# A graph network on one core: the last pass in another order, and twelve tiles kept in SBUF between two passes

## What is computed

```python
h = (x @ W.T).reshape(N, 4, 64)
e = leaky_relu(a_s[src] + a_d[dst], 0.2)        # edges and a loop at each node
p = exp(e - m[dst]);  alpha = p / (segment_sum(p, dst) + 1e-16)
out = segment_sum(alpha[:, :, None] * h[src], dst).reshape(N, 256) + bias
x = layernorm(elu(out) + x + x)
```

## Time and profile before

| | |
|---|---|
| runs of the kernel before | 5779.85 us median of 3 (5770.6 to 5787.17) |
| the profiled execution | 5752.64 us, span 5750.9 us |
| busy in the span | PE 4250.1 us, DVE 3705.5, POOL 3618.8, ACT 1959.4 |
| DMA | 1129.62 MB moved, mean 196 GB/s |
| mean granted TensorE clock | 0.873 |

### The profile page before, as it was taken

How to read it: one execution, slowest core, us unless ns; L and a number is a source line. 1 busy time by engine, 2 the same in 40 slices (tenths; PEclk the granted TensorE clock), 3 DMA queues, 4 the chain that set the end, 5 groups by cost and what they waited for, 6 DMA issues and landing times. The chain is left out here.

```text
span 5750.9 us, 69994 instructions
## 1 busy us (share of the span) xinstructions
PE 4250.1 (74%) x16758; PEld 2855.9 (50%) x16758; DVE 3705.5 (64%) x10203; ACT 1959.4 (34%) x3345; POOL 3618.8 (63%) x3319
## 2 busy tenths in 40 slices
PE   2377679999999999999999777767777400026776
PEld 1255445556666666666666566656666300012222
DVE  1255456566666666666666566668888645558887
ACT  0011145532222222222222222227777300016666
POOL 7488644433556666555555566657777776668887
PEclk7688889999999999999999887778999755559888
DMA  9988799984433333333333233339999522249997
GB/s 378 283 154 153 139 303 365 363 313 148 142 121 123 123 123 123 122 121 119 118 119 111 90 124 122 123 119 317 325 325 324 197 88 81 86 137 352 350 347 286
DMA packets 497174, 1129.62 MB, mean 196 GB/s; under 512 B 164006, under 2 KB 246906, under 8 KB 497030
## 3 DMA queue, kind: packets, MB, share of 16 engines
q1 hardware_dynamic: 331530, 866.20, 43.1%
q0 software_dynamic: 113184, 174.84, 12.5%
q10 hardware_dynamic: 52316, 87.06, 4.3%
HBM read 627.40 MB, written 543.83 MB: 204 GB/s over the span
## 5 line engine op out<-in xcount | busy, mean ns | idle before, releaser
L1067 PE MATMUL psum<-W2b,arena 128*128 128x256 f32 x3136 | 725.2, 379 | 0.0
L799 DVE TENSOR_SCALAR arena<-arena 128x256 f32<-128x256 f32 x784 | 463.0, 653 | 369.4 <-POOL arena L794 364.9
L1048 PE MATMUL psum<-arena,W1b 128*128 128x512 f32 x1568 | 699.1, 599 | 0.0
L1067 PEld LDWEIGHTS psum<-W2b,arena 128*128 128x128 f32 x3136 | 573.1, 190 | 66.3 <-issue 0.5
L1761 PE MATMUL psum<-arena,ident 128*128 128x512 f32 x784 | 418.8, 685 | 194.7 <-POOL arena L1819 192.4
L959 ACT ACTIVATE arena<-psum,hbias 128x512 f32<-128x512 f32 x392 | 269.5, 687 | 809.6 <-PE psum L1048 809.6
L1192 POOL DMA_INDIRECT tab<-arena,IDX x392 | 408.9, 1043 | 190.4 <-issue 114.0
L1610 POOL DMA_INDIRECT ad_d<-arena,FE x392 | 406.9, 1038 | 156.1 <-issue 127.4
L1048 PEld LDWEIGHTS psum<-arena,W1b 128*128 128x128 f32 x1568 | 289.8, 190 | 402.4 <-issue 402.4
L790 POOL TENSOR_TENSOR arena<-arena,lneps 128x4 f32<-128x4 f32 x196 | 42.0, 215 | 668.3 <-DVE arena L786 667.5
L1251 PE MATMUL psum<-ident,arena 128*128 128x128 f32 x24 | 5.7, 424 | 590.4 <-DVE arena L1419 581.1
(11 more groups left out here) (256 smaller groups left out, 9269.0 us busy)
## 6 DMA issues: line engine op xcount, KB each, us to landing
arena<-tab SPq DMA_DIRECT2D x194, 544.0 KB
arena<-x_d SPq DMA_DIRECT2D x202, 512.0 KB
arena<-in_x SPq DMA_DIRECT2D x194, 512.0 KB
x_d<-arena SPq DMA_DIRECT2D x194, 512.0 KB
tab<-zero SPq DMA_DIRECT2D x11, 5832.0 KB
tab<-blank SPq DMA_DIRECT2D x97, 544.0 KB
h_d<-arena SPq DMA_DIRECT2D x97, 528.0 KB
arena<-h_d SPq DMA_DIRECT2D x97, 528.0 KB
```

Source lines behind the costliest of these rows:

```text
L799: v.tensor_scalar(y[:, j, :], r[:, j, :], self.mv[:, j, 0:1], self.rs[:, j:j + 1], ALU.subtract, ALU.mult).then_inc(self.s["y"], 1)
L1048: last = pe.matmul(psum[:, HB[c], :], W1b[:, f, c * P:(c + 1) * P], x1T[:, f, :], start=False, stop=(f == FH - 1))
L1067: last = pe.matmul(outB(j), hid[:, c, j * P:(j + 1) * P], W2b[:, c, :], start=(c == 0), stop=(c == KH - 1))
```

## The change

**Kept tiles.** The weights and the two constant tiles get a place at the end of one large array, and from phase four on twelve tiles of [128, 4, 256] lie where they and some unused room were. In `edge_pass(2)` SyncE loads into tile m the x2 rows of step 8m (m = 0 to 11). `node_pass` reads the rows of these steps there and doesn't load them. In steps 8m + 4 ScalarE copies `y` into tile m, and `y` isn't stored to `x3_d`; `last_pass` reads these steps' rows from tile m and doesn't load them. The loops of these two passes get bodies of eight steps in place of four where slots of eight matter.

**The last pass in another order.** TensorE does the two matmuls of `oh`, for which it waits alone, then the two of `oS`. The residual sum `rr` has four buffers and not two. `factors` and `shares` are cut into seven pieces, `heads`, `slopes`, `maxima`, `below`, `sums`, `totals`, `shares`, which VectorE does at different places of its body. The negated mean of step k (`negated`) moves behind the elu of step k + 1.

The diff, cut to its core:

```diff
+        NKEEP, TILE = 12, J * D
+        KEEP0 = ARENA - 5 * TILE
+        arena = sb("arena", [P, KEEP0 + NKEEP * TILE + J * TW - TILE])
+        kept = arena[:, KEEP0:KEEP0 + NKEEP * TILE].rearrange("p (m j d) -> p m j d", m=NKEEP, j=J)
...
+        EVERY = 2 * NB
+        KFULL = NS // EVERY
+        assert KFULL == NKEEP and NS % EVERY == 2
+
+        def found(k):
+            return k.i % EVERY == 0 and not (k.known() and k.s >= EVERY * NKEEP)
+
+        def stays(k):
+            return k.i % EVERY == NB
+
+        def sent(k):
+
+            b = k.slot(NB)
+            if b:
+                return 32 * k.turn(NB) + 16 * USES[b]
+            return 16 * (3 * k.m + (2 if k.i else 0)) + 16 * USES[0]
+
+        SENT = [48 * USES[b] - (16 * NKEEP if b == 0 else 0) for b in range(NB)]
+        READ = [16 * (2 * USES[b] - (NKEEP if b == 0 else 0)) for b in range(NB)]
...
+                for s in range(S0, S0 + NG):
+                    body(beat(s, NG))
+                for m in range(NKEEP):
+                    a, n = node_view(x2_d, at(EVERY * m))
+                    sp.dma_start(kept[:, m, :, :], a).then_inc(p3_fill, 16)
+                run_beats(sp, CS - NG, body, NG, start=S0 + NG)
                 ahead["rows", L](sp)
+                sp.wait_ge(p3_fill, 16 * (NS + NKEEP))
...
+            def xtile(k):
+                return kept[:, k.m, :, :] if found(k) else xt[:, k.slot(NB), :, :]
+
+            def read(k):
 
                 b = k.slot(NB)
-                wait(eng, n_w[b], 32 * k.turn(NB) + 16 * USES[b])
+                if b:
+                    return 16 * (k.turn(NB) + USES[b] + 1)
+                return 16 * (k.m + USES[0] + 1)
 
             def rows(sp, k):
-                b = k.slot(NB)
+                if found(k):
+                    return
                 wait(sp, r["r"], k.s - NB + 1)
                 a, n = node_view(xin, k)
-                sp.dma_start(xt[0:n, b, :, :], a).then_inc(n_x[b], 16)
+                sp.dma_start(xt[0:n, k.slot(NB), :, :], a).then_inc(n_x[k.slot(NB)], 16)
...
             def n_sync(sp):
                 def store(k):
                     b = k.slot(NB)
+                    if stays(k):
+                        return
                     sp.wait_ge(r["y"], J * (k.s + 1))
...
+                    if stays(k):
+                        act.wait_ge(r["y"], J * (k.s + 1))
+                        act.wait_ge(r["r"], k.s - NB + 1)
+                        act.activation(kept[:, k.m, :, :], y[:, k.slot(NB), :, :], ACT.Copy).then_inc(s_c["id"], 1)
...
+                    if not found(k):
+                        v.wait_ge(n_x[k.slot(NB)], read(k))
                     wait(v, r["y"], J * (k.s - NB + 1))
-                    v.tensor_tensor(out=rr[:, k.slot(NB), :, :], in0=xt[:, k.slot(NB), :, :], in1=unit, op=ALU.add).then_inc(r["r"], 1)
+                    v.tensor_tensor(out=rr[:, k.slot(NB), :, :], in0=xtile(k), in1=unit, op=ALU.add).then_inc(r["r"], 1)
...
-            rr = take([2, J, D])
+            rr = take([NB, J, D])
...
+            def xtile(k):
+                return kept[:, k.m, :, :] if stays(k) else xt[:, k.slot(NB), :, :]
+
+            def read(k):
+
+                b = k.slot(NB)
+                return READ[b] + 16 * ((k.turn(NB) if b else k.m) + 1)
+
             def rows(sp, k):
                 b = k.slot(NB)
+                if stays(k):
+                    return
...
             def l_tensor(pe):
                 def body(k):
                     b = 2 * k.slot(NB)
-                    pe.wait_ge(r["oS"], k.s + 1)
-                    pe.wait_ge(r["oh"], k.s + 1)
                     wait(pe, r["r"], k.s + Z - NB + 1)
-                    for i in range(2):
-                        for n, a in enumerate((oh, oS)):
+                    for n, (a, made) in enumerate(((oh, "oh"), (oS, "oS"))):
+                        pe.wait_ge(r[made], k.s + 1)
+                        for i in range(2):
                             last = pe.matmul(psum[:, b + i, :], ident[:, :], a[:, k.slot(2), 2 * i:2 * i + 2, :].rearrange("p j d -> p (j d)"),
                                              start=(n == 0), stop=(n == 1))
...
             def l_vector(v):
-                def factors(k):
-
-                    p = k.turn(2)
-                    c0 = 6 * p
+                def heads(k):
                     for n in (k, k.plus(1)):
                         b = n.slot(NB)
                         v.wait_ge(gd[b], 16 * (n.turn(NB) + GD[b] + 1))
                         v.wait_ge(n_t[b], 16 * (n.turn(NB) + 2 * USES[b] + 1))
-                    M = pair_cols(tt, k, MC)
                     v.tensor_tensor(out=l1, in0=pair_cols(ht, k, D), in1=pair_cols(ht, k, D + H), op=ALU.add).then_inc(r["small"], 1)
-                    v.wait_ge(r["small"], c0 + 1)
+
+                def slopes(k):
+                    v.wait_ge(r["small"], 6 * k.turn(2) + 1)
                     v.scalar_tensor_tensor(out=es, in0=l1, scalar=SLOPE, in1=l1, op0=ALU.mult, op1=ALU.max).then_inc(r["small"], 1)
-                    v.wait_ge(r["small"], c0 + 2)
-                    v.tensor_tensor(out=top, in0=M, in1=es, op=ALU.max).then_inc(r["small"], 1)
-                    v.wait_ge(r["small"], c0 + 3)
+
+                def maxima(k):
+                    v.wait_ge(r["small"], 6 * k.turn(2) + 2)
+                    v.tensor_tensor(out=top, in0=pair_cols(tt, k, MC), in1=es, op=ALU.max).then_inc(r["small"], 1)
+
+                def below(k):
+                    p = k.turn(2)
+                    v.wait_ge(r["small"], 6 * p + 3)
                     wait(v, r["w"], p)
-                    v.tensor_tensor(out=dd[:, 0, :, :], in0=M, in1=top, op=ALU.subtract).then_inc(r["d"], 1)
+                    v.tensor_tensor(out=dd[:, 0, :, :], in0=pair_cols(tt, k, MC), in1=top, op=ALU.subtract).then_inc(r["d"], 1)
                     v.tensor_tensor(out=dd[:, 1, :, :], in0=es, in1=top, op=ALU.subtract).then_inc(r["d"], 1)
 
+                def sums(k):
+                    v.wait_ge(r["w"], k.turn(2) + 1)
+                    v.tensor_tensor(out=t1, in0=pair_cols(tt, k, SC), in1=ww[:, 0, :, :], op=ALU.mult).then_inc(r["small"], 1)
+
+                def totals(k):
+                    v.wait_ge(r["small"], 6 * k.turn(2) + 4)
+                    v.scalar_tensor_tensor(out=den, in0=t1, scalar=1e-16, in1=ww[:, 1, :, :], op0=ALU.add, op1=ALU.add).then_inc(r["small"], 1)
+
                 def shares(k):
-                    p = k.turn(2)
-                    c0 = 6 * p
-                    v.wait_ge(r["w"], p + 1)
-                    v.tensor_tensor(out=t1, in0=pair_cols(tt, k, SC), in1=ww[:, 0, :, :], op=ALU.mult).then_inc(r["small"], 1)
-                    v.wait_ge(r["small"], c0 + 4)
-                    v.scalar_tensor_tensor(out=den, in0=t1, scalar=1e-16, in1=ww[:, 1, :, :], op0=ALU.add, op1=ALU.add).then_inc(r["small"], 1)
-                    v.wait_ge(r["small"], c0 + 5)
+                    v.wait_ge(r["small"], 6 * k.turn(2) + 5)
                     v.reciprocal(den, den).then_inc(r["small"], 1)
-                    v.wait_ge(r["small"], c0 + 6)
+                    v.wait_ge(r["small"], 6 * k.turn(2) + 6)
                     wait(v, r["oS"], k.s - 2)
                     v.tensor_tensor(out=cc[:, k.slot(NB) // 2, :, :, :].rearrange("p i j h -> p i (j h)"), in0=ww.rearrange("p i j h -> p i (j h)"),
                                     in1=den.rearrange("p (a j) h -> p a (j h)", a=1).to_broadcast([P, 2, 2 * J * H]), op=ALU.mult).then_inc(r["cc"], 1)
 
+                def negated(k):
+                    b = k.slot(2)
+                    v.wait_ge(r["mv"], J * (k.s + Z + 1))
+                    wait(v, r["nm"], k.s + ZP - 1)
+                    v.tensor_scalar(neg[:, b, :], mv[:, b, :, 0], -1.0, None, ALU.mult).then_inc(r["neg"], 1)
+
                 for s in (0, 2):
-                    factors(beat(s, NB))
-                    shares(beat(s, NB))
+                    for part in (heads, slopes, maxima, below, sums, totals, shares):
+                        part(beat(s, EVERY))
 
                 def body(k):
-                    b = k.slot(2)
+                    b, b4 = k.slot(2), k.slot(NB)
+                    even = b == 0 and live(k.plus(4), NS)
+                    odd = b == 1 and live(k.plus(3), NS)
                     v.wait_ge(r["ex"], k.s + Z + 1)
                     v.scalar_tensor_tensor(out=banks(k), in0=ex[:, b, :, :], scalar=-1.0, in1=banks(k), op0=ALU.add, op1=ALU.max).then_inc(r["elu"], 1)
+                    if not (k.known() and k.s == 0):
+                        negated(k.plus(-1))
+                    if even:
+                        heads(k.plus(4))
                     v.wait_ge(r["elu"], k.s + 2 * Z + 1)
-                    v.wait_ge(n_x[k.slot(NB)], 16 * (k.turn(NB) + 2 * USES[k.slot(NB)] + 1))
-                    wait(v, r["y"], J * (k.s + Z - 1))
```

(62 more changed lines are left out.)

42 lines of the change are left out of this document (22 added, 20 removed).

## The result

| | before | changed |
|---|---|---|
| median of 5 runs, us | 5779.85 (5770.6 to 5788.94) | 5892.16 (5888.57 to 5895.07) |
| ratio, with 95% interval | | 1.0193 (1.0179 to 1.0206) |
| span of the profiled execution, us | 5750.9 | 5890.4 |

The kernel became 112 us slower; the forecast was 5886. The stages, read from the marks that GpSimd makes at the barriers, show where: the last pass took 617.9 us and takes 724.6; the node pass 673.7 and 686.3; the two edge passes 629.3 and 640.7, 586.0 and 597.6, of which the second isn't touched by the change.

The account below looks back on a forecast made before the run. The prediction took transfers to pace the node pass and a ring of VectorE, GpSimd, TensorE and ScalarE the last pass; -34 + 2 + 138 = +106 us on a median of 5779.85 gave 5886 us, range 5800 to 5965.

Parts of the forecast that it names:

- The step in the last pass: Last pass: a mean of 7.5 us a step against 6.09, odd bodies 6.8 and even ones 8.2.
- term of +138 us: Last pass: the new order makes two waits that add 1.41 us to each of 98 steps.
- The table wait: Last pass, even bodies: `heads` waits for a table landing at 1.45 us at the earliest, and is released at 2.2.
- late table: Rival, last pass: the table lands after the first product, 8.2 us a step, +175 us, total 5955; chance 0.15.
- The port: Last pass: a small VectorE operation with two SBUF inputs, issued during a GpSimd product, costs the rest of that product.
- The node pass: Node pass: 6.0% fewer bytes through kept tiles give -34 us, bounds -38 and +13.
- transfers pace that pass: Node pass: VectorE's 44.3 us of waits at L1629 are for stores to land; full pacing makes 6.0% worth 38 us.
- The edge pass: Edge pass ahead of the node pass: the 12 loads that come back there cost +2 us, between nothing and 18.
- The sum: Whole kernel: -34 + 2 + 138 = +106 us, forecast 5886 us.

Follow-up runs that it names:

- order alone: The kernel before with the last pass in the changed order and no kept tiles: 5710.4 against 5604.1 us, ratio 1.0192.
- repeated trace: The kernel before, unchanged, run and traced once more on another chip: 5603.63 us.
- port experiment: The kernel before plus one small VectorE operation behind each last-pass residual sum: ratio 1.0149 with two SBUF inputs, 0.9992 with one in PSUM.

## Why the prediction was right, step by step

**The step in the last pass.** Forecast 7.5 us (6.8 for odd bodies, 8.2 for even ones), measured 7.22 (6.23 and 8.52 in the median; in the pair shown 8.50, and 6.61 and 6.23 for the odd ones beside it). The term of +138 us measured +106 (order alone). Both mechanisms were the ones named.

**The table wait** was right as a mechanism, with a size of its own wrong: I took the latency of a lone load, 4.07 us, and had the table land inside the first product. In the pair shown `heads` started 5.57 us after the issue (5404.51 to 5410.08), inside the second; over the 47 pairs behind the pass's beginning it was 4.84 us in the median (3.89 to 7.01), inside the second product in 32, inside the first in 10. That is the rival "late table" in two pairs of three, with its place but not its price: I had 9.6 us for that even body, since my bodies held gaps that aren't there. Where VectorE's instructions stand ready behind one another they start 1.13 us apart although each takes 1.22 (L1965 at 5410.94, L1912 at 5412.07). The two errors cancel in part, and this is luck.

**The port** was right, and shown by itself. `slopes` isn't blocked in the median, as the table's delay put it behind the second product; `sums` and `totals` are blocked for longer than I had (1139 and 623 ns, I had 0.9 and 0.4 us). Of the order's 106 us the place of the wait makes some 70, by the run that moves it alone. The other 36 go with the places of the operations, and 29 of them vanish where these stand together. A part of these 29 is waiting, as `heads` waited for the heads' rows where only the table wait had been moved (39.9 us); how much is blocked time wasn't measured apart.

**The node pass** was wrong: -34 us, measured -9 by the traces on the two chips that are alike, none on the slower ones, and nothing in the total. The step that failed is "transfers pace that pass". It rested on a reading: VectorE waits 44.3 us at L1629 for "remote", "that is for stores to land (`out_wait`)". The code of `to_rows` has `out_wait` only ahead of the first of its two operations; ahead of the second it waits for TensorE's matmuls alone:

```python
out_wait(v, k)
wait(v, s_xd[b], 16 * J * k.turn(NB) + XD3[b])
for i in range(2):
    v.wait_ge(r["mm"], 2 * k.s + i + 1)
    v.tensor_tensor(out=hs[:, b, 2 * i:2 * i + 2, :], ...
```

25 of the 33 waits, 30.8 of the 44.3 us, stand ahead of the second, as here in the kernel before:

```profile
3993.57 0.71 DVE L1629 TENSOR_TENSOR arena<-psum,bias 128x528 f32<-128x528 f32 x1 [0.98 <-PE psum L1555]
3995.07 0.71 DVE L1629 TENSOR_TENSOR arena<-psum,bias 128x528 f32<-128x528 f32 x1 [0.80 <-remote]
```

And each of the 33 ends with an update of the semaphore that L1555, the matmul, counts up; none ends with a landing. "remote" only means that the profile didn't find the instruction that released the wait. So the pass was a ring of engines, and it had no wait for a transfer that could be shortened. In the repeated trace these waits don't occur at all. The prediction also weighed VectorE's and ScalarE's time in this pass and not GpSimd's: 459.51 of 600 us look like room, but the 0.30 us before each indirect transfer aren't counted as busy. With them GpSimd had 483.6 of 500 us in that trace (3900 to 4400 us):

```profile
L1610 POOL DMA_INDIRECT ad_d<-arena,FE x304 | 316.8, 1042 | 117.7 <-issue 100.9 <-DVE arena L1629 13.5 <-DVE arena L1664 3.4
L1604 POOL TENSOR_TENSOR arena<-arena,expo 128x8 f32<-128x8 f32 x38 | 65.9, 1735 | 0.3
```

**The edge pass**: +2, measured +5.

**The sum** came within 6 us of the result because the terms' errors balance: last pass 32 us too dear, node pass some 25 to 34 too cheap. The direction and the last pass's two waits are the prediction's own; the closeness is luck.

## What to carry to other kernels

A small VectorE operation with two inputs in SBUF was cheap here only where none of GpSimd's long products ran: it belongs into the stretch in which GpSimd is idle or at small work, and one moved into a "gap" took nine times its own time (1646 ns against 181). When a piece with a wait is moved ahead, count from the issue of what it waits for, at the latency of a loaded queue, and put each wait at the first operation that needs it. Before bytes are taken out of a pass with a DMA share near 1, add up each engine's busy time and its issue gaps: where one engine's sum is the whole window, look there first. And before a wait for "remote" is called a transfer, read in the code which semaphores that very instruction waits for.

## What the runs showed of the hardware that was not expected

- A VectorE operation of 128x32 with two SBUF inputs took 1646 ns in the median beside GpSimd's products of 1901 ns, with one input in PSUM 181 ns. GpSimd's products weren't lengthened by it (two in 3.76 us in the changed kernel, as before). Beside GpSimd's power of 128x4 (1.01 us) small operations kept their 0.19 us, as in both kernels of the port experiment.
- GpSimd's indirect transfers come one every 1.3 us where it is full: 1.02 us of work and 0.30 us that the profile calls idle.
- A DMA share of 0.99 to 1.01 stood beside steps that 6% fewer bytes didn't shorten.
- A load of 544 KB was used 4.84 us after its issue in the median at a DMA share of 0.83; the earlier trace rows had 6.5 us at 0.94.
- The same kernel took 5601 to 5604 us and 5780 to 5788 us on different chips; the last pass differs little and the node pass more (621.8 and 656.1 us against 617.9 and 673.7), the edge passes by 68 and 66 us.
